# Attention outputs transposed in 32x32 blocks on VectorE instead of on TensorE, in a three-attention block on one core

## The chip, the core and the metric

The kernel runs as one program on one core of a Trainium2 chip. The core's engines run their own instruction queues and meet at semaphores: PE (TensorE, matrix products; PEld is its weight load), DVE (VectorE), ACT (ScalarE), POOL (GpSimd) and SP (SyncE, which here only issues DMAs). The metric is the device time of one execution in microseconds (us), lower is better.

## The reference

A batch of 16 sequences of 512 tokens with 128 channels goes through two layers, in fp32:

```python
x = L0_attn_x                                   # 16 x 512 x 128
xn = layernorm(x)
x = x + L0_attn(xn) + L0_ffn(xn)
xn = layernorm(x)
return x + L1_attn(xn) + L1_ffn(xn)
```

`L0_attn` ("A" in the kernel) has 16 query heads of 8 channels over 4 key/value heads, without a mask. `L0_ffn` contains a second attention ("M": 16 heads, keys and values from a normalised latent, rotary positions, causal) and then a mixture of 4 experts of which each token takes one. `L1_attn` ("B") has 16 query heads over one key/value head. `L1_ffn` is a gated feed-forward of width 384. Each attention computes `softmax(q k^T) v` per head, puts the heads' 8 channels side by side and multiplies by an output matrix `wo`.

## The kernel before, in words

One table of steps, written out by hand, sets the order of all work. `T` (L119) gives each step a place on a time axis, `stages` (L139) lists the steps of one sequence with their places, `ordered` (L225) folds the places modulo `PERIOD = 12` and sorts them, and each engine walks the folded table once per sequence, doing its own part of each step (`walk`, L434). So up to three sequences are in work at once, and the loop over sequences has 12 slots. `LATE` (L128) shifts a step on one engine alone. A place is only a rank: an engine's instructions run strictly in the order of the table, and wait there on semaphores.

The attentions take turns. In each slot one group of 4 heads is scored for its row maxima (`score_max`, L687 on PE, L956 on DVE), and another group, two slots behind, is scored again with the maximum folded in, exponentiated (`score_exp`, L707 on PE, L1201 on ACT) and multiplied with the values (`probs_v`, L723, PE). For A and B a group has 16 score_max units, each four matmuls in four column tiles into one PSUM bank and one DVE reduction of 128x512 (L966); for M the tiles grow with the causal row, and a masked reduction (L971) takes them. The slots with score_max of A are 8 to 11, of B 0 to 3, of M 4 to 7. The maxima go through POOL, PE, ACT and a DMA issued by SP (`shift_turn`, L560, L701, L1194) before the second scoring of that group.

PSUM has 8 banks: 7 that all score units and all small products take in turn (`misc_bank`, L604, waits for the last user of a bank), and one, `pv`, in which `probs_v` collects a pair of groups. After a pair of groups (twice per attention, so six times per sequence):

- `out_copy` (L1210): ACT copies `pv` (128x512) to `osb`. The `pv` bank is free again after it: `probs_v` of the next pair waits for it.
- `out_turn` (L742, L974): PE transposes `osb` in four 128x128 pieces into a PSUM bank, so that tokens lie on partitions; DVE takes the reciprocal of the row sums (L979) and multiplies (L986) into `otok`.

And once per attention, three times per sequence:

- `o_turn` (L749, L1216): PE transposes `otok` back in four 128x128 pieces, ACT copies the bank to `oT`; then `o_proj` (L754) multiplies with `wo`, and DVE adds the result (L998, L1002, L1006).

Other steps that the change moves: `m_lat_turn` (L646, L913: DVE normalises the latent, PE transposes it, DVE scales it), `gate`, `route` (L1032) and `scatter` (L1386) of the experts' routing, the POOL chains `split` with the nine `pack` DMAs behind each (L569), and the feed-forward `ff_up`, `ff_down`.

Of the kernel before, what the change touches and what calls it, by code (L numbers as in the profile page):

```python
# [31 lines left out]
ALU = mybir.AluOpType  # L32
# [3 lines left out]
P = 128  # L36
# [3 lines left out]
GROUP = 4  # L40
# [61 lines left out]
for _n, _w in (("a_bv", 32), ("a_bo", 128), ("gate_b", EXPERTS), ("b_bv", HD), ("b_bo", 128)):  # L102
# [16 lines left out]
T = dict(x_load=-0.9, x_norm=-0.066, res0=1.148, x_scaled=0.46, turn_xr=0.9, m_q=1.107, split_mq=1.25, m_lat=0.995,  # L119
         m_lat_turn=1.55, m_k=1.763, split_mk=1.85, m_v=1.95, turn_xn=2.283, a_q=2.542, split_aq=2.687, a_k=2.8,  # L120
         a_v=3.432, split_ak=3.649, pack=0.319, pack_a=1.414,
         nms=1.16, nmT=1.5, lag=1.986, pv_M=3.114, pv=3.265, out_copy=1.188, out_turn=0.125, o_turn=0.222, o_proj=0.382,
         x2_norm=0.352, e0=13.6, x2_scaled=-0.691, turn_r2=-0.5, gate=-0.318, ranks=0.157, route=0.15, route_step=0.043, scatter=0.75, xp_in=1.58, xp_turn=2.314, weights=1.15, wgap=0.209, wnext=0.2, up=2.849, step=0.248, later=0.3,
         y_out=0.25, gather=0.618, moe_added=1.272, down=0.03,
         b0=0.12, x1_scaled=0.177, res1=0.75, turn_x1=0.513, b_q=0.801, split_bq=0.18, b_k=1.03, split_bk=0.195, b_v=1.248,
         ff=1, ff_down=0.358)

LATE = {  # L128
    "SP": dict(shift_turn=0.067),
    "PE": dict(),  # L130
    "DVE": dict(o_proj=0.024, x1_scaled=0.022, m_lat_turn=0.0, x_scaled=-0.121, m_lat=0.0, x1_norm=0.0, x2_norm=0.0,
                down=0.0, out_turn=0.0, gate=0.0),
    "ACT": dict(turn=-0.056, out_copy=-0.063, o_turn=0.0, x_scaled=0.0, x2_scaled=0.0, shift_turn=0.017, m_v=0.0, up=-0.013),
    "POOL": dict(x_norm=0.106, x1_norm=0.184, x2_norm=0.042, m_lat=0.1, gate=0.1, m_q=0.069, m_k=0.05,
                 split=0.0, score_exp=0.0),
# [96 lines left out]
def spare_users(name, *args):  # L232
# [8 lines left out]
        "out_turn": [(f"{a}_otok", g + 1)] if name == "out_turn" else [],  # L241
        "o_turn": [(f"{a}_oT", 1)], "o_proj": [({"M": "x2_ready", "A": "gqa_added", "B": "y_ready"}.get(a), 1)],
# [12 lines left out]
def kernel_program(nc, x, w_all, w_lat, v_all, r_all, consts, wx, xq, yq, wi_up, wi_down, rope, out):  # L255
# [7 lines left out]
    with ctx:  # L263
# [63 lines left out]
        otok = sb("otok", [P, TILES, D])  # L327
# [63 lines left out]
        for a in "MBA":  # L391
# [206 lines left out]
        def _(pe):  # L598
# [143 lines left out]
            def out_turn(b, a, g):  # L742
                m = misc_bank(b, f"{a}_otok", g + 1)
                pe.wait_ge(sig[f"{a}_osb"], total(b, f"{a}_osb", g + 1))
                for t in range(TILES):
                    ins = pe.transpose(m[:, P * t:P * t + P], osb[:, g % 2, P * t:P * t + P], ident[:])  # L746
                ins.then_inc(sig[f"{a}_ot_ps"], 1)

            def o_turn(b, a):  # L749
                m = misc_bank(b, f"{a}_oT", 1)  # L750
                pe.wait_ge(sig[f"{a}_otok"], total(b, f"{a}_otok"))
                turns4(m, otok, f"{a}_oT_ps")

# [63 lines left out]
            def ff_down(b):  # L817
                m = misc_bank(b, "res_b", 1)
                pe.wait_ge(sig["ff_hid"], total(b, "ff_hid"))
                for t in range(TILES):  # L820
                    for c in range(FCH):
# [6 lines left out]
                         shift_turn=shift_turn, score_exp=score_exp, probs_v=probs_v, out_turn=out_turn,  # L828
                         o_turn=o_turn, o_proj=o_proj, gate=gate, ranks=ranks, xp_turn=xp_turn, up=up, down=down, ff_up=ff_up, ff_down=ff_down)
# [4 lines left out]
        def _(v):  # L834
            turn_mx, turn_full, turn_otok, turn_factored = {}, {}, {}, {}
            turn_hid = {}
# [279 lines left out]
            def ff_down(b):  # L1116
# [13 lines left out]
                         score_max=score_max, out_turn=out_turn, o_proj=o_proj,  # L1130
# [6 lines left out]
        def _(act):  # L1137
            turn_probs, turn_osb, turn_oT, turn_nmT, turn_factored = {}, {}, {}, {}, {}
# [71 lines left out]
            def out_copy(b, a, g):  # L1210
                act.wait_ge(sig[f"{a}_pv"], total(b, f"{a}_pv", len(CLUSTERS[a]) * (2 * g + 2)))
                for s_last, value in last_user(b, turn_osb, g % 2, f"{a}_ot_ps", g + 1):
                    act.wait_ge(s_last, value)
# [283 lines left out]
```

## Time and profile before

| | |
|---|---|
| median of 3 runs | 2818.49 us (2809.54 to 2819.48) |
| span of the profiled execution, first to last instruction | 2813.9 us |
| PE busy | 2628.6 us, 93% |
| PEld busy | 1437.3 us, 51% |
| DVE busy | 2305.2 us, 82% |
| ACT busy | 1727.4 us, 61% |
| POOL busy | 791.1 us, 28% |

The profiled execution is one of its own; of its time the trace has the span alone, which lies inside the range of the three runs and 4.6 us under their median. Matmuls overlap and their ends are modelled, so PE's busy time is an upper bound. The profile follows each idle stretch of an engine to the instruction that released it.

### The profile page before, as it was taken

The numbers are of one execution on the slowest core, as the hardware profiler recorded it, in microseconds if no ns is written. First come the engines' busy times: TensorE is split into PE (matmuls) and PEld (weight loads), VectorE is DVE, ScalarE is ACT, GpSimd is POOL, SyncE is SP. The second block draws the span as 40 slices with busy tenths as digits, with TensorE's granted clock in tenths as the row PEclk, the third lists the DMA queues.
The fourth block names the chain that finished last, engine by engine and source line by source line (L and its number), as shares of the span: only waits on it lengthen the run. The fifth ranks groups of instructions, "written<-read, shape, count | busy, mean of one in ns | idle before, by whom it ended". The sixth has DMA issues, their size and how long they took to land. (4 is left out here: it accounts for less than half of the span.)

```text
span 2813.9 us, 121706 instructions
## 1 busy us (share of the span) xinstructions
PE 2628.6 (93%) x51440; PEld 1437.3 (51%) x51440; DVE 2305.2 (82%) x6003; ACT 1727.4 (61%) x3522; POOL 791.1 (28%) x1369
## 2 busy tenths in 40 slices
PE   5969999999999999999999999999999999999958
PEld 2435454645546465464645546464554646546432
DVE  5758879798898979889797988979889897988825
ACT  1725756666576666757666575766657566675725
POOL 4132422223241222423223242222324122242110
PEclk7979999999999999999999999999999999999987
DMA  3041221403112041221304122140312214132120
GB/s 98 7 125 36 79 76 32 125 25 108 55 59 89 26 135 30 89 73 36 113 25 123 43 77 79 31 125 25 110 52 67 81 29 133 29 90 73 34 71 6
DMA packets 168048, 191.30 MB, mean 68 GB/s; under 512 B 24614, under 2 KB 150736, under 8 KB 167504
## 3 DMA queue, kind: packets, MB, share of 16 engines
q1 hardware_dynamic: 163408, 175.12, 20.4%
q0 software_dynamic: 4096, 8.40, 1.0%
q8 instruction: 406, 6.65, 1.0%
q14 instruction: 138, 1.13, 0.1%
HBM read 84.18 MB, written 16.25 MB: 36 GB/s over the span
## 5 line engine op out<-in xcount | busy, mean ns | idle before, releaser
L1208 ACT ACTIVATE probs<-bank 128x512 f32<-128x512 f32 x2688 | 1463.7, 599 | 678.2 <-PE bank L615 670.6
L966 DVE TENSOR_REDUCE mx<-bank 128x1 f32<-128x512 f32 x2048 | 1281.2, 682 | 62.4 <-PE bank L615 49.3
L971 DVE CUSTOM_DVE_ANT_0 bank<-bank,mask 128x128 f32<-128x128 f32 (+3 forms) x1024 | 478.5, 517 | 109.2 <-PE bank L615 101.7
L615 PE MATMUL bank<-kp_B,qp_B 72*32 72x512 bf16 x4096 | 439.9, 390 | 18.5 <-DVE mx L966 9.2
L615 PE MATMUL bank<-qp_B,kp_B 74*32 74x512 bf16 x4096 | 413.5, 382 | 3.1 <-ACT probs L1208 1.7
L615 PE MATMUL bank<-qp_A,kp_A 74*32 74x512 bf16 x4096 | 408.5, 380 | 6.8 <-DVE mx L966 6.2
L615 PE MATMUL bank<-kp_A,qp_A 72*32 72x512 bf16 x4096 | 394.8, 381 | 12.4 <-DVE mx L966 7.5
L615 PE MATMUL bank<-kp_M,qp_M 72*32 72x128 bf16 (+3 forms) x4096 | 318.4, 311 | 32.0 <-DMA kp_M<-parts_k 23.5
L1353 POOL TENSOR_SCALAR nms<-mx 128x16 bf16<-128x16 f32 x192 | 39.5, 206 | 1087.1 <-DVE mx L971 509.6
L615 PE MATMUL bank<-qp_M,kp_M 74*32 74x128 bf16 (+3 forms) x4096 | 297.5, 302 | 20.0 <-DVE mx L966 15.2
L736 PE MATMUL pv<-probs,vv_B 128*32 128x512 f32 x2048 | 274.8, 594 | 1.2 <-ACT probs L1208 1.0
L736 PE MATMUL pv<-probs,vv_A 128*32 128x512 f32 x2048 | 266.6, 593 | 0.1
L615 PEld LDWEIGHTS bank<-kp_B,qp_B 72*32 72x32 bf16 x4096 | 133.4, 97 | 207.0 <-issue 86.3
L615 PE MATMUL bank<-late_keys,identb 128*32 128x128 bf16 x4096 | 221.1, 221 | 0.9 <-issue 0.8
L615 PEld LDWEIGHTS bank<-qp_B,kp_B 74*32 74x32 bf16 x4096 | 129.8, 97 | 133.7 <-issue 51.7
L615 PEld LDWEIGHTS bank<-qp_A,kp_A 74*32 74x32 bf16 x4096 | 122.4, 97 | 147.4 <-DVE mx L966 42.6
L615 PEld LDWEIGHTS bank<-kp_A,qp_A 72*32 72x32 bf16 x4096 | 115.2, 96 | 146.4 <-DVE mx L966 58.9
L615 PEld LDWEIGHTS bank<-qp_M,kp_M 74*32 74x32 bf16 x4096 | 130.8, 97 | 108.1 <-DVE mx L966 40.0
L615 PEld LDWEIGHTS bank<-kp_M,qp_M 72*32 72x32 bf16 x4096 | 126.1, 99 | 108.3 <-issue 56.8
L736 PE MATMUL pv<-probs,vv_M 128*32 128x512 f32 (+3 forms) x2048 | 179.3, 437 | 0.2
L615 PEld LDWEIGHTS bank<-late_keys,identb 128*32 128x32 bf16 x4096 | 129.8, 98 | 50.1 <-issue 29.3
L971 DVE DVE_READ_ACCUMULATOR2_ANT mx<- 128x1 f32 x1024 | 145.2, 142 | 0.0
(167 smaller groups left out, 3286.4 us busy)
## 6 DMA issues: line engine op xcount, KB each, us to landing
wxs<-wx SPq DMA_DIRECT2D x112, 578.0 KB, 4.1
qp_M<-parts_q SPq DMA_DIRECT2D x144, 128.0 KB
kp_M<-parts_k SPq DMA_DIRECT2D x144, 128.0 KB
qp_A<-parts_q SPq DMA_DIRECT2D x144, 128.0 KB
qp_B<-parts_q SPq DMA_DIRECT2D x144, 128.0 KB
xp<-xq SPq DMA_DIRECT2D x16, 448.0 KB, 7.3
kp_A<-parts_k SPq DMA_DIRECT2D x144, 32.0 KB
xs<-x SPq DMA_DIRECT2D x16, 256.0 KB, 3.0
```

What stands on the lines that cost most here:

```text
L615: ins = pe.matmul(dst[at:at + n], lhsT[:, at:at + n], rhs, start=start, stop=stop, tile_position=(0, at))
L736: ins = pe.matmul(pv[0][32 * hh:32 * hh + VW, SEQ - q:SEQ], vv[a][:, c, VHEAD[a](GROUP * g + hh), :], probs[:, SLOT[a, g, u], col:col + q] ...
L966: v.tensor_reduce(mx[:, g % 2, at:at + 1], s1[BANK[a, g, u]][:], AX.X, ALU.max) \
L971: v.tensor_tensor_reduce(bank[:, 0:keys], bank[:, 0:keys], mask[:, SEQ - keys:SEQ], 1.0, LOWEST, ALU.add, ALU.max, mx[:, g % 2, at:at + 1] ...
L1208: act.activation(probs[:, slot, :], s2[BANK2[a, g, u]][:], ACT.Exp).then_inc(sig[f"{a}_exp"], 1)
L1353: chain(b, f"{a}_nms", 2 * g + 1, pool.tensor_scalar(first, top, 1.0, 0.0, ALU.mult, ALU.add))
```

## The change

The `pv` tile is transposed by DVE, and so is `otok`, each in one instruction over 128x512 that turns every 32x32 block in place. Head pairs lie on blocks of 32 partitions, so the blocks are enough: between the two transpositions a token's place within its block lies on the partition. The division reads `osb` in SBUF instead of a PSUM bank. PE and ACT have no part in `out_copy`, `out_turn` and `o_turn` any more, and the nine uses of the turning banks per sequence are gone. The rows of `wo` are put in another order on the host.

```diff
-        "out_turn": [(f"{a}_otok", g + 1)] if name == "out_turn" else [],
-        "o_turn": [(f"{a}_oT", 1)], "o_proj": [...
+        "o_proj": [...
...
-        otok = sb("otok", [P, TILES, D])
+        otok = sb("otok", [P, SEQ])
...
 # on PE: out_turn and o_turn are taken out
-            def out_turn(b, a, g):
-                m = misc_bank(b, f"{a}_otok", g + 1)
-                pe.wait_ge(sig[f"{a}_osb"], total(b, f"{a}_osb", g + 1))
...
-            def o_turn(b, a):
...
 # on DVE
+            def out_copy(b, a, g):
+                v.wait_ge(sig[f"{a}_pv"], total(b, f"{a}_pv", len(CLUSTERS[a]) * (2 * g + 2)))
+                for s_last, value in last_user(b, turn_osb, g % 2, f"{a}_otok", g + 1):
+                    v.wait_ge(s_last, value)
+                v.transpose(osb[:, g % 2, :], pv[0][:]).then_inc(sig[f"{a}_osb"], 1)
+
             def out_turn(b, a, g):
-                v.wait_ge(sig[f"{a}_ot_ps"], total(b, f"{a}_ot_ps", g + 1))
-                m = misc[SPARE[f"{a}_otok", g + 1]][:].rearrange("p (t h c) -> p t h c", t=TILES, c=VHALF)
+                v.wait_ge(sig[f"{a}_osb"], total(b, f"{a}_osb", g + 1))
+                m = osb[:, g % 2, :].rearrange("p (k h c) -> p k h c", h=2, c=VHALF)
...
                 v.reciprocal(r, m[:, :, :, HD]).then_inc(sig[f"{a}_rc"], 1)
...
+                dst = otok[:].rearrange("p (k g h d) -> p k g h d", g=TWOS, h=2, d=HD)[:, :, g]
+                v.tensor_tensor(dst, m[:, :, :, 0:HD], r.unsqueeze(3).broadcast_to([P, SEQ // TILE, 2, HD]), ALU.mult) \
+                    .then_inc(sig[f"{a}_otok"], 1)
+
+            def o_turn(b, a):
+                v.wait_ge(sig[f"{a}_otok"], total(b, f"{a}_otok"))
+                for s_last, value in last_user(b, turn_oT, 0, f"{a}_o_ps", 1):
+                    v.wait_ge(s_last, value)
+                v.transpose(oT[:], otok[:]).then_inc(sig[f"{a}_oT"], 1)
...
 # on ACT: out_copy and o_turn are taken out
-                act.activation(osb[:, g % 2, :], pv[0][:], ACT.Copy).then_inc(sig[f"{a}_osb"], 1)
...
-                act.activation(oT[:], misc[SPARE[f"{a}_oT", 1]][:], ACT.Copy).then_inc(sig[f"{a}_oT"], 1)
```

The steps' places also change. In `T` (before, after; the others stay):

```
turn_xr 0.9 0.81    m_q 1.107 1.103      m_lat 0.995 0.943   m_k 1.763 1.724     split_mk 1.85 1.774
m_v 1.95 1.813      res0 1.148 1.007     x_load -0.9 -0.923  x_scaled 0.46 0.579 a_k 2.8 2.963
a_v 3.432 3.374     split_ak 3.649 3.654 nmT 1.5 1.422       o_turn 0.222 0.162  e0 13.6 13.621
turn_r2 -0.5 -0.399 route_step 0.043 0.053  xp_turn 2.314 2.341  weights 1.15 1.141  wgap 0.209 0.168
moe_added 1.272 1.279  turn_x1 0.513 0.459  b_q 0.801 0.601  split_bq 0.18 0.281  b_k 1.03 1.118
split_bk 0.195 0.245   b_v 1.248 1.83       ff 1 1.199       ff_down 0.358 0.346
```

and `LATE` becomes

```python
    "SP": dict(shift_turn=0.351, y_out=0.008, xp_in=0.021, pack=0.082),
    "PE": dict(m_v=-0.035, o_proj=-0.027, m_lat_turn=0.123, b_v=-0.004, ranks=-0.104, a_q=-0.077, turn=-0.047,
               down=-0.019),
    "DVE": dict(o_proj=0.024, x1_scaled=0.022, x_scaled=-0.121, x2_norm=-0.155, down=-0.031, out_turn=0.131,
               route=0.1, m_q=0.001, x_norm=0.039),
    "ACT": dict(turn=-0.037, out_copy=-0.081, x_scaled=0.01, shift_turn=0.017, up=-0.013, a_k=0.291, b_q=0.501),
    "POOL": dict(x_norm=0.051, x1_norm=0.184, x2_norm=0.042, m_lat=0.1, gate=-0.056, m_q=0.069, m_k=-0.063,
               res1_start=-0.147, scatter=-0.042, res0_start=0.015),
```

(before: SP `shift_turn=0.067`; PE nothing; DVE `o_proj`, `x1_scaled`, `x_scaled` as now and zeros; ACT `turn=-0.056, out_copy=-0.063, shift_turn=0.017, up=-0.013`; POOL `x_norm=0.106, x1_norm=0.184, x2_norm=0.042, m_lat=0.1, gate=0.1, m_q=0.069, m_k=0.05`). Folded to the 12 slots, PE's part of `m_lat_turn` goes from 2.550 to 2.673 while DVE's stays at 2.550; the expert gate's POOL part goes ahead of the `split` of M's queries; SP's part of `shift_turn` goes 0.2 slots back, behind `pack` or `weights` issues in slots 2, 3, 6 and 10; the feed-forward goes 0.2 slots back.

## Rows read from the trace of the kernel before

**Rows 1.** The page: span; busy time by engine, share, instructions.
```profile
span 2813.9 us, 121706 instructions
PE 2628.6 (93%) x51440; PEld 1437.3 (51%) x51440; DVE 2305.2 (82%) x6003; ACT 1727.4 (61%) x3522; POOL 791.1 (28%) x1369
```
**Rows 2.** Timeline, DVE: start, length, one instruction that runs once per sequence, ten apart.
```profile
492.55 0.45 DVE L1052 TENSOR_TENSOR past<-first_row,cst 1x21 f32<-1x21 f32 x1
2160.63 0.45 DVE L1052 TENSOR_TENSOR past<-first_row,cst 1x21 f32<-1x21 f32 x1
```
**Rows 3.** Windows, slots 0-2, 2-4, 4-8, 8-12: length; PE, PEld, DVE, ACT, POOL busy.
```profile
1449.90:1474.10 24.20, 23.32 (x366) 10.72 (x362) 22.91 (x47) 19.70 (x43) 3.81 (x11) 1.00 0.01 2
1474.10:1507.60 33.50, 32.32 (x563) 16.38 (x552) 30.32 (x70) 20.70 (x43) 21.39 (x32) 1.00 0.28 84
1507.60:1561.10 53.50, 52.35 (x1305) 34.95 (x1307) 39.08 (x157) 34.41 (x73) 8.45 (x16) 1.00 0.43 133
1561.10:1616.70 55.60, 53.80 (x1014) 27.40 (x1010) 51.29 (x105) 33.05 (x63) 15.23 (x26) 1.00 0.12 33
```
**Rows 4.** Waits in 1561.1 to 1616.7: who waited for whom, us, times, longest.
```profile
PEld bank L615 <- DVE mx L966: 7.3, 17, 1.1
DVE res L1119 <- PE bank L615: 1.5, 1, 1.5
```
**Rows 5.** Timeline, 1508.0 to 1512.6: one end of a pair of groups.
```profile
1509.88 0.60 ACT L1214 ACTIVATE osb<-pv 128x512 f32<-128x512 f32 x1 [0.29 <-PE pv L736]
1510.63 0.63 PE L746 MATMUL bank<-ident,osb 128*128 128x128 f32 x4 [0.21 <-ACT osb L1214]
1511.19 0.29 PE L615 MATMUL bank<-kp_M,qp_M 72*32 72x256 bf16 x4
```
**Rows 6.** Timeline, PE, 1483 to 1486: the transposition of the latent.
```profile
1485.14 0.60 PE L650 MATMUL bank<-ident,latn 128*64 128x128 f32 x4 [1.18 <-DVE latn L859]
```
**Rows 7.** Timeline, DVE, 1480 to 1487: four reductions in a row.
```profile
1481.59 2.47 DVE L966 TENSOR_REDUCE mx<-bank 128x1 f32<-128x512 f32 x4
```
**Rows 8.** Groups by line: count, busy us, mean ns, idle before.
```profile
L1214 ACT ACTIVATE osb<-pv 128x512 f32<-128x512 f32 x96 | 57.3, 597 | 61.8 <-PE pv L736 61.7
L1220 ACT ACTIVATE oT<-bank 128x512 f32<-128x512 f32 x48 | 28.0, 584 | 15.2 <-PE bank L621 15.2
L1096 DVE TENSOR_TENSOR acc<-acc,moe 128x512 f32<-128x512 f32 x16 | 10.9, 682 | 9.1 <-DMA moe<-yq,row_at_i 9.1
L923 DVE TENSOR_SCALAR latT<-bank,vec 64x512 f32<-64x512 f32 x16 | 12.8, 801 | 12.9 <-PE bank L650 12.9
```
**Rows 9.** Timeline, SP, 1483 to 1508: DMA issues.
```profile
1484.96 6.01 SPq L584 DMA_DIRECT2D qp_M<-parts_q  x9
1501.79 1.21 SPq L566 DMA_DIRECT2D qp_B<-nmT  x2
```
**Rows 10.** DMA issues of the whole span: KB each, median us to landing.
```profile
xp<-xq SPq DMA_DIRECT2D x16, 448.0 KB, 7.3
qp_A<-nmT SPq DMA_DIRECT2D x128, 4.0 KB, 1.7
```
**Rows 11.** Timelines, POOL, SP and PE, 1480 to 1522: routing, scatter and what reads it.
```profile
1484.16 0.20 POOL L1378 TENSOR_SCALAR oneh<-eq 128x4 f32<-128x4 f32 x1
1485.87 0.20 POOL L1384 TENSOR_TENSOR oneh<-eq,seen 128x4 f32<-128x4 f32 x1
1499.37 1.11 POOL L1394 DMA_INDIRECT xq<-factored,row_at_i  x1 [1.95 <-DVE row_at_i L1072]
1508.06 0.39 SPq L530 DMA_DIRECT2D xp<-xq  x1
1518.04 0.66 PE L788 MATMUL bank<-ident,xp 128*128 128x128 f32 x4
```
**Rows 12.** Timeline, 2800 to 2814: the end of the last sequence.
```profile
2805.24 0.60 ACT L1214 ACTIVATE osb<-pv 128x512 f32<-128x512 f32 x1 [1.19 <-PE pv L736]
2809.02 1.54 PE L615 MATMUL bank<-w,oT 128*32 128x128 f32 x32 [0.78 <-ACT oT L1220]
```

More of the change, by code:

```diff
@@ L115 @@
             "B": ((0, 4), (4, 8), (8, 12), (12, 16))}
[L119 to L126, printed above, removed]
@@ L128 @@
-LATE = {
[L129 to L135, printed above, removed]
+T = dict(x_load=-0.923, x_norm=-0.066, res0=1.007, x_scaled=0.579, turn_xr=0.81, m_q=1.103, split_mq=1.25,
+         m_lat=0.943, m_lat_turn=1.55, m_k=1.724, split_mk=1.774, m_v=1.813, turn_xn=2.283, a_q=2.542,
+         split_aq=2.687, a_k=2.963, a_v=3.374, split_ak=3.654, pack=0.319, pack_a=1.414, nms=1.16, nmT=1.422,
+         lag=1.986, pv_M=3.114, pv=3.265, out_copy=1.188, out_turn=0.125, o_turn=0.162, o_proj=0.382, x2_norm=0.352,
+         e0=13.621, x2_scaled=-0.691, turn_r2=-0.399, gate=-0.318, ranks=0.157, route=0.15, route_step=0.053,
+         scatter=0.75, xp_in=1.58, xp_turn=2.341, weights=1.141, wgap=0.168, wnext=0.2, up=2.849, step=0.248,
+         later=0.3, y_out=0.25, gather=0.618, moe_added=1.279, down=0.03, b0=0.12, x1_scaled=0.177, res1=0.75,
+         turn_x1=0.459, b_q=0.601, split_bq=0.281, b_k=1.118, split_bk=0.245, b_v=1.83, ff=1.199, ff_down=0.346)
@@ L240, in spare_users @@
         "shift_turn": [(f"{a}_nmT", g + 1)] if name == "shift_turn" else [],
-        "out_turn": [(f"{a}_otok", g + 1)] if name == "out_turn" else [],
-        "o_turn": [(f"{a}_oT", 1)], "o_proj": [({"M": "x2_ready", "A": "gqa_added", "B": "y_ready"}.get(a), 1)],
+        "o_proj": [({"M": "x2_ready", "A": "gqa_added", "B": "y_ready"}.get(a), 1)],
         "gate": [("logits", 1)],
@@ L827, in _ @@
                          a_q=a_q, a_k=a_k, a_v=a_v, b_q=b_q, b_k=b_k, b_v=b_v, score_max=score_max,
-                         shift_turn=shift_turn, score_exp=score_exp, probs_v=probs_v, out_turn=out_turn,
-                         o_turn=o_turn, o_proj=o_proj, gate=gate, ranks=ranks, xp_turn=xp_turn, up=up, down=down, ff_up=ff_up, ff_down=ff_down)
+                         shift_turn=shift_turn, score_exp=score_exp, probs_v=probs_v, o_proj=o_proj, gate=gate, ranks=ranks, xp_turn=xp_turn, up=up, down=down, ff_up=ff_up, ff_down=ff_down)
             walk(steps, ordered(LATE["PE"]))
@@ L1129, in _ @@
                          b_v=lambda b: value(b, "B", "b_ps", "b_bv", "bv_ready"),
-                         score_max=score_max, out_turn=out_turn, o_proj=o_proj,
+                         score_max=score_max, out_copy=out_copy, out_turn=out_turn, o_turn=o_turn, o_proj=o_proj,
                          x2_norm=x2_norm, gate=gate, route=route, up=up, down=down, moe_added=moe_added,
@@ L1208, in score_exp @@
                 act.activation(probs[:, slot, :], s2[BANK2[a, g, u]][:], ACT.Exp).then_inc(sig[f"{a}_exp"], 1)
[L1210 to L1213, printed above, removed]
-                act.activation(osb[:, g % 2, :], pv[0][:], ACT.Copy).then_inc(sig[f"{a}_osb"], 1)
-            def o_turn(b, a):
-                act.wait_ge(sig[f"{a}_oT_ps"], total(b, f"{a}_oT_ps"))
-                for s_last, value in last_user(b, turn_oT, 0, f"{a}_o_ps", 1):
-                    act.wait_ge(s_last, value)
-                act.activation(oT[:], misc[SPARE[f"{a}_oT", 1]][:], ACT.Copy).then_inc(sig[f"{a}_oT"], 1)
             def xp_turn(b, half):
@@ L1251, in _ @@
                            m_v=m_v, shift_turn=shift_turn,
-                           score_exp=score_exp, out_copy=out_copy, o_turn=o_turn, xp_turn=xp_turn, up=up,
+                           score_exp=score_exp, xp_turn=xp_turn, up=up,
                            ff_up=ff_up), ordered(LATE["ACT"]))
@@ L1434 @@
     k_at = {"A": HD * (np.arange(KCH["A"]) % KV0) + np.arange(KCH["A"]) // KV0, "B": np.arange(KCH["B"])}
[L1436 removed]
+    head, pair, odd, ch_of = np.unravel_index(np.arange(D), (GROUP, TWOS, 2, HD))
     o_at = HD * (GROUP * (2 * pair + odd) + head) + ch_of
```

21 lines of the change are left out of this document (4 added, 17 removed).

## The prediction, made before the changed kernel was built or run

> **What bounds the kernel now.** I read the page first: PE is busy 93% of the span, DVE 82%, ACT 61% [rows 1]. Then the length of a period: one DVE instruction that runs once per sequence stands at 492.55 and, ten sequences on, at 2160.63, so a period is 166.8 us [rows 2]. The reader is to see next, in the windows of one period, that the bound is not the same everywhere [rows 3]. In slots 4 to 8 PE is busy 52.35 of 53.5 us while DVE idles 14.4 and ACT 19.1: PE alone sets the pace. In the other three stretches (113.3 us together) PE is busy 109.4, but DVE is busy 104.5 and idles only 8.8 (1.3, 3.2 and 4.3), and PE waits for it: 7.3 us on its weight loads in slots 8 to 12, always for a reduction that has to free a bank [rows 4]. There two engines are nearly full side by side. The change takes work from the one and gives it to the other.
>
> The Trainium skill ("Trainium Kernel Development and Optimization", Performance Expectations) calls matmul busy time a bad measure and weight-load busy time a good one. By that PE, at 51%, would be far from its limit and lose nothing by these transpositions. In slots 4 to 8 the trace speaks against it: no other engine is near full there. It stands behind the rival of no change.
>
> **What PE loses.** Nine sets of four transpositions per period: six `out_turn`, three `o_turn`. From the start of one set to the next product 0.56 us pass (1510.63 to 1511.19) [rows 5]; 9 x 0.56 = 5.0 us. By their places: one set in slots 0 to 2, two in 2 to 4 (A's last), three in 4 to 8 (B's last), three in 8 to 12 (M's last).
>
> **What ACT loses.** Nine copies of 0.60 us, 5.3 us per period [rows 8]. ACT idles in every stretch [rows 3]; taken as nothing, at most the 0.21 us that PE stood before a set [rows 5].
>
> **What DVE gains.** Nine transpositions over 128x512, six from PSUM, three from SBUF. The trace has none, so I bound it by other instructions of that size: reductions from PSUM follow each other at 0.60 us ((2.47 - 0.68) / 3, the last one taken as long as a lone instruction of that size) [rows 7]; an addition in SBUF takes 0.68 alone, and the slowest one of 512 columns, a scaling from PSUM, 0.80 [rows 8]. I take 0.60, as the nearest in kind (one source from PSUM, one element after the other, in a queue): 5.4 us per period, 0.6, 1.2, 1.8 and 1.8 by stretch. That a block needs more than one pass is the last rival below. The division keeps its 32 and 256 elements and reads SBUF in place of PSUM: nothing, within 0.1 us either way.
>
> On this price the Trainium skill has a rule ("VectorE: DVE Perf Modes", The three transpose paths): 311 ns on VectorE for 128x128, 390 on TensorE, and its rules for authors give a 128x128 transposition to TensorE. Four times 311 is 1.24 us by that page, an estimate, twice my 0.60, and by it the change costs DVE 11.2 us. No run so far shows it.
>
> **The sum by stretch.** Slots 4 to 8: PE gives back 3 x 0.56 = 1.7 us, and DVE's 39.1 + 1.8 stays far below 51.8; -1.7.
>
> The other three: PE falls to 109.4 - 6 x 0.56 = 106.1, and with its present idle time of 3.9 the stretches could shrink to 110.0. DVE rises to 104.5 + 3.6 = 108.1, and with its present idle time of 8.8 they would grow to 116.9. What decides is how much of DVE's idle time is slack. A part are waits on PE that get shorter when DVE runs later than PE (1.5 us before adding the feed-forward's result [rows 4]); a part are hand-overs in chains (latent, feed-forward) that stay. I let half stay: 108.1 + 4.4 = 112.5; -0.8.
>
> **The places.** `m_lat_turn`: PE stands 1.18 us before it, for DVE's normalised latent [rows 6]. Its PE part goes 0.123 slots back, in slots of 16.75 us (33.5 / 2 [rows 3]) 2.1 us; but on DVE two new instructions (1.2 us) come ahead of it in that slot. So 0.3 of the wait could stay and 0.9 go. Behind it `m_k` now follows closer, and waits for the scaled latent, an instruction of 0.80 [rows 8]. I take -0.4, with bounds of 0 and -0.9.
>
> SP's part of `shift_turn`, two DMAs: for B's third group it was issued from 1501.79 to 1503.00 [rows 9] and lands 1.7 us after [rows 10], 2.9 before slot 4 opens at 1507.6, where PE reads it. Now the last two packs (6.01 / 9 = 0.67 each [rows 9]) and two weight loads go ahead of it, some 2 us. 0.9 is left, so nothing; without that cover PE would wait 1 to 2 us per period. In the other slots what goes ahead is less or the slot longer.
>
> POOL's gate, seven instructions from 1484.16 to 1486.07 [rows 11], goes ahead of the split of M's queries, and the nine packs behind it end some 2 us later than 1490.97 [rows 9], for a slot that opens at 1507.6: nothing. The twelve `route` steps spread up to 0.23 slots further back, 3.9 us; POOL's scatter, which waits for the last of them already (1.95 us), follows, then the load of the sorted rows, which lands 7.3 us [rows 10] after 1508.06, at 1515.4, 2.7 before PE reads it at 1518.04 [rows 11]. PE's reading goes back by 0.05 slots, 0.8. That is 3.5 against 3.9: nothing taken, up to +0.4. Feed-forward 0.2 slots back: in the half above. `b_v`, 0.58 back, is read four slots later.
>
> **The new wait.** In `out_copy` DVE waits for PE's last product into `pv`, with its reductions queued behind, and PE needs the banks that they free. ACT stood so 61.7 us over 96 copies, 0.64 each [rows 8]. I count nothing extra, since DVE in the full stretches arrives late, not early, and in slots 4 to 8 has room. The other way, PE's next pair waits until DVE has emptied `pv`. Its first product lies 0.235 slots behind `out_copy` in the table for A and B, some 3 us in slots of 12 to 14 us; DVE, at most some four reductions (2.4 us) behind before PE runs out of banks, and 0.6 for the transposition, just keeps that.
>
> **Total.** -1.7 - 0.8 - 0.4 = -2.9 us per period. 15 periods stand between the 16 sequences: -43.5. At the very end, where nothing covers the chain from 2805.24 to the last projection at 2809.02 [rows 12], two sets and two copies (2 x (0.63 + 0.60) [rows 5]) give way to two transpositions of 0.68: -1.1. 2813.9 - 44.6 = 2769.3 for the span; the median of the runs is 4.6 us above the span shown: 2774.
>
> **The rivals.**
> - PE alone counts: DVE's new work disappears in its idle time, the three stretches shrink to 110.0 and the latent's wait by 0.9. -1.7 - 3.3 - 0.9 - 0.4 (ACT's copies no longer waited for) = -6.3, so 2723. For it: PE is at 93% everywhere. Against: PE waits for DVE's reductions already.
> - No change: 6.5 of DVE's 8.8 us turn out to be hand-overs; the three stretches grow by 1.3, which with the latent's 0.4 eats the 1.7: 2817.
> - Slower: DVE stands at `pv` as ACT did, 0.64 us at each of four ends outside slots 4 to 8, 2.6 us, so that its idle time stays at 8.8 although it runs later. 116.9 in place of 113.3, the latent's wait unchanged: +3.6 - 1.7 = +1.9 per period, 2846. It turns slower from the point where 6.9 us of idle time stay. For it: ACT's idle time before the copies was all for PE [rows 8]. Against: [rows 4].
> - A transposition takes two passes, 1.20 us: DVE 111.7 in the three stretches, with half the idle time 116.1, +2.8, -1.7 in slots 4 to 8, the latent's wait stays: +1.1, 2834. By the skill's 1.24 it would be the same within 5 us.
>
> **Chances.** Forecast 0.50, with a range of its own of 2737 to 2803 (a quarter to three quarters of DVE's idle time stay); PE alone 0.14; no change 0.15; DVE at `pv` 0.12; two passes 0.09. 0.5%, 14 us, is what a measurement here can tell from no change. Faster by more: 0.46 of the forecast, 0.14, and 0.05 of the third, 0.65. Within: 0.04 + 0.08 + 0.04 of the slower ones, 0.16. Slower: 0.19. The range runs from 2720, which takes in most of the second case, to 2840, between the two slow ones.
>
> **What would show it.** Right: DVE busy up by some 5 us per period to about 149, transpositions at 0.60 to 0.70, PE down to about 157 of 164; slots 4 to 8 near 51.8 us, the others near 112; no wait of PE for `osb` above some tenths. Wrong: transpositions above 1 us; DVE idle before `out_copy` for PE's product; PE idle before the second scoring for a DMA of `nmT`; slots 8 to 12 longer than 55.6; or slots 4 to 8 unchanged, which would mean that PE was not their bound.

## The result and the profile after

The changed kernel takes 2825.64 us (median of 20 runs), the kernel before in the same runs 2817.38: ratio 1.0031, 95% interval 1.0021 to 1.0040. 2774 us had been forecast; it became slightly slower. The page of the changed kernel, span and busy times [rows 1]:

```profile
span 2829.3 us, 120408 instructions
PE 2587.7 (91%) x50864; PEld 1427.0 (50%) x50864; DVE 2377.3 (84%) x6147; ACT 1692.9 (60%) x3378; POOL 799.1 (28%) x1369
```

The work moved: PE has 41 us less, DVE 72 more. Yet the span is 15 us longer, so PE stands more. Windows of one period of the changed kernel, the same four stretches [rows 3]; the number before the DMA share is the granted clock:

```profile
1457.60:1482.00 24.40, 23.31 (x362) 9.51 (x362) 23.29 (x48) 19.59 (x41) 5.06 (x12) 1.00 0.01 3
1482.00:1514.60 32.60, 30.50 (x542) 14.28 (x535) 30.73 (x71) 20.52 (x42) 17.62 (x28) 1.00 0.28 84
1514.60:1571.50 56.90, 51.09 (x1301) 34.99 (x1297) 41.27 (x162) 33.38 (x71) 11.59 (x19) 1.00 0.42 125
1571.50:1626.20 54.70, 51.97 (x998) 28.46 (x991) 52.49 (x107) 32.15 (x60) 15.09 (x25) 1.00 0.12 33
```

Slots 2 to 4 and 8 to 12 are 0.9 us shorter each, slots 4 to 8 are 3.4 longer, though PE is busy 1.3 less there. Taken as means over 11 periods, from the first `score_max` product of a slot to that of the next, the period goes from 166.8 to 167.9: slots 0 to 2 from 24.2 to 24.5, 2 to 4 from 33.7 to 33.1, 4 to 8 from 53.2 to 55.3, 8 to 12 from 55.6 to 54.9. The loss sits in slot 4 (11.5 to 13.7) and slot 6 (18.5 to 18.7, where it should have shrunk). All slot and period lengths below are such means; a wait "per period" is the time by which PE's products start later than those before them allow, by what released them, over 12 periods.

Waits of the whole span of the changed kernel (us, times, longest) name two candidates:

```profile
PEld bank L613 <- DMA qp_B<-nmT: 32.1, 17, 3.1
PE bank L613 <- DMA qp_B<-nmT: 23.9, 15, 2.5
PE bank L613 <- DMA wxs<-wx: 22.4, 30, 1.8
DVE osb L964 <- PE pv L734: 45.9, 50, 14.7
PE bank L648 <- DVE latn L845: 24.9, 16, 3.1
```

The wait for B's `nmT` is new, and the one for the expert weights `wxs` was shorter before:

```profile
PE bank L615 <- DMA wxs<-wx: 8.7, 9, 1.9
```

The chain of waits of the changed kernel goes through that shift DMA once in nearly every period (14 such steps, 3.6 to 7.1 us); two of them:

```profile
1514.11 4.01 DMA qp_B<-nmT
2344.88 4.85 DMA qp_B<-nmT
```

The operations themselves are near the forecast (groups of DVE: count, busy us, mean ns, idle before; the mean is that of a whole instruction, which in a queue runs into the next one):

```profile
L964 DVE STREAM_TRANSPOSE osb<-pv 128x512 f32<-128x512 f32 x96 | 68.3, 711 | 45.9 <-PE pv L734 45.9
L984 DVE STREAM_TRANSPOSE oT<-otok 128x512 f32<-128x512 f32 x48 | 33.8, 703 | 0.1
L977 DVE TENSOR_TENSOR otok<-osb,rc 128x256 f32<-128x256 f32 x96 | 44.1, 460 | 3.3
L971 DVE RECIPROCAL rc<-osb 128x32 f32<-128x32 f32 x96 | 32.8, 342 | 0.1
```

### The profile page after: what moved, and what is told of

It is laid out like the page before. It is cut to its first block, busy times and chain, and to the rows that moved or that the text cites. A ratio compares the mean times of both kernels' runs of the same rounds, so it can differ in the third digit from the quotient of the medians.

```text
span 2829.3 us, 120408 instructions
## 1 busy us (share of the span) xinstructions
PE 2587.7 (91%) x50864; PEld 1427.0 (50%) x50864; DVE 2377.3 (84%) x6147; ACT 1692.9 (60%) x3378; POOL 799.1 (28%) x1369
## 3 DMA queue, kind: packets, MB, share of 16 engines
q1 hardware_dynamic: 163408, 175.12, 20.6%
## 4 chain that ended last, share of the span: by engine, by line
PE 45%; DVE 29%; issue 7%; SPq 7%; DMA 6%; POOL 5%; ACT 2%; POOLq 0%; DVEq 0%; ACTq 0%
PE bank L613 33%; DVE mx L952 16%; PE pv L734 10%; SPq L582 4%; DMA wxs<-wx 3%; DMA qp_B<-nmT 2%; SPq L536 2%; DVE bank L957 1%; ACT probs L1204 1%; DVE osb L964 1%; POOL sq L1282 1%; DVE bn L827 1%; PE bank L619 1%; DVE oT L984 1%; DVE latn L845 1%
## 5 line engine op out<-in xcount | busy, mean ns | idle before, releaser
L613 PE MATMUL bank<-kp_B,qp_B 72*32 72x512 bf16 x4096 | 421.8, 391 | 18.7 <-DVE mx L952 9.8
L613 PE MATMUL bank<-qp_A,kp_A 74*32 74x512 bf16 x4096 | 417.1, 382 | 8.8 <-DVE mx L952 8.2
L613 PE MATMUL bank<-kp_A,qp_A 72*32 72x512 bf16 x4096 | 403.5, 383 | 6.7 <-DVE mx L952 3.4
L613 PE MATMUL bank<-kp_M,qp_M 72*32 72x128 bf16 (+3 forms) x4096 | 327.6, 317 | 32.7 <-issue 27.6
L613 PE MATMUL bank<-qp_M,kp_M 74*32 74x512 bf16 (+3 forms) x4096 | 299.9, 305 | 17.7 <-DVE mx L952 15.8
L613 PEld LDWEIGHTS bank<-qp_A,kp_A 74*32 74x32 bf16 x4096 | 128.1, 96 | 186.7 <-DVE mx L952 106.1
L613 PEld LDWEIGHTS bank<-kp_M,qp_M 72*32 72x32 bf16 x4096 | 132.3, 101 | 110.2 <-issue 72.2
L613 PEld LDWEIGHTS bank<-kp_A,qp_A 72*32 72x32 bf16 x4096 | 122.7, 96 | 119.1 <-DVE mx L952 42.5
L613 PE MATMUL bank<-xpT,wxs 128*32 128x128 f32 x3584 | 124.6, 277 | 26.6 <-DMA wxs<-wx 22.4
```

Of the source, the lines that this page charges most:

```text
L613: ins = pe.matmul(dst[at:at + n], lhsT[:, at:at + n], rhs, start=start, stop=stop, tile_position=(0, at))
```

## The experiments

### Exchange and places apart

**e1**: the changed code with the old places.

```diff
-T = dict(x_load=-0.923, ...   # after
+T = dict(x_load=-0.9, ...     # before
-LATE = ...                    # after
+LATE = ...                    # before
```

> The transpositions are on VectorE as in the changed kernel, but all steps have the places of the kernel before (T and LATE of before). Theory P (the exchange of engines gains what was forecast, the new places take it back): PE's stalls return from 17.1 to about 12 us per period, the waits for DMA nmT (1.9), for the expert weights (1.4), for POOL's nms (1.0) go to a few tenths; time 2760 to 2785, ratio to before about 0.98 to 0.99. Theory D (DVE is the bound, and its 5.4 us of new work eat the 5.0 us that PE loses, whatever the places): 2810 to 2835, ratio 1.00 +- 0.005, and the stalls of PE on DVE's reductions rise by 3 us per period or more.

2881.29 us, ratio 1.0259 (1.0238 to 1.0280). The period is 171.6, and nearly all of the loss lies in slot 2, 20.6 to 24.9. Neither theory had this: with the old places the exchange loses.

**e2**: the code of before with the new places.

```diff
-T, LATE = ...   # before
+T, LATE = ...   # after
```

> The transpositions stay on PE and ACT as in the kernel before, but all steps have the new places (T and LATE of the changed kernel). Theory P: the new places by themselves cost some 3 to 5 us per period, 2860 to 2895. Theory D: the places are about neutral, 2810 to 2830.

2883.82 us, 1.0254 (1.0230 to 1.0278). In the kernel before the two waits below come to 9.0 and 2.2 us. DVE's division frees the turning bank, and with the new places it comes later:

```profile
PEld bank L616 <- DVE otok L987: 80.0, 74, 1.8
PE bank L616 <- DVE otok L987: 49.3, 74, 1.4
```

Each half alone costs some 2.5%, together 0.3%: the places belong to the exchange, and no part of the result can be read as one half's share.

**e7**: e1 with `m_lat_turn`'s new place on PE.

```diff
-    "PE": dict(),
+    "PE": dict(m_lat_turn=0.123),
```

> e1_old_places (transpositions on VectorE, all places as before) with a single new place: PE's part of m_lat_turn 0.123 slots back, as in the changed kernel. Theory L (with the old places the whole loss is in slot 2, where DVE's three new steps of A come ahead of the latent and PE and DVE wait for each other in turn): slot 2 falls from 24.9 to 21 us, ratio to before 0.997 to 1.005. Theory D (DVE's load is the loss): no change, 1.02 or more.

2853.60 us, 1.0127 (1.0108 to 1.0145): half of e1's loss, between the two expectations. Slot 2 falls from 24.9 to 22.4.

### How much PE and DVE count

**e4**: the kernel before, each of the nine sets of PE transpositions done twice.

```diff
-                for t in range(TILES):
+                for t in (*range(TILES), *range(TILES)):
```

> The kernel before, with each of the nine sets of four PE transpositions per period done twice into the same place: prices PE's part. If 0.56 us of PE work per set is what the time pays (PE bound everywhere): 9 x 0.56 x 15 = +76 us, 2893. If only slots 4 to 8 are bound by PE: 3 x 0.56 x 15 = +25, 2842. If PE has room: 2817.

2854.20 us, 1.0158 (1.0136 to 1.0180). 5.0 us of PE work per period lengthen it by 2.1, 43%. The three sets in slots 4 to 8, 1.7 us, make that stretch 0.5 longer. In slot 6 PE's busy time grows by 0.7 and the slot by 0.1: PE is not its bound.

**e8**: e5 (below) with `out_copy`'s transposition done twice.

```diff
+                v.transpose(unused[:, g % 2, :], pv[0][:])
                 v.transpose(osb[:, g % 2, :], pv[0][:])...
```

> e5_shift with out_copy's transposition done twice (once into a tile that nothing reads): prices six DVE transpositions per period, 6 x 0.6 = 3.6 us. If DVE's time is on the path in slots 0 to 4 and 8 to 12, four of six count: +2.4 us per period, +36 us on e5_shift. If everywhere: +54. If DVE has room: within 10 us.

2822.29 us, 1.0030 (1.0016 to 1.0043), 28 above e5. In a queue one takes 673 ns, alone 711; from the start of the first to that of the second pass 0.64 us:

```profile
L965 DVE STREAM_TRANSPOSE unused<-pv 128x512 f32<-128x512 f32 x96 | 68.2, 711 | 33.3 <-PE pv L735 33.3
L966 DVE STREAM_TRANSPOSE osb<-pv 128x512 f32<-128x512 f32 x96 | 64.6, 673 | 0.0
```
```profile
1454.18 0.72 DVE L965 STREAM_TRANSPOSE unused<-pv 128x512 f32<-128x512 f32 x1 [0.25 <-PE pv L735]
1454.82 0.67 DVE L966 STREAM_TRANSPOSE osb<-pv 128x512 f32<-128x512 f32 x1
```

The period grows by 2.2 of the 3.8 added (6 x 0.64), 2.0 of it outside slots 4 to 8, where four of the six lie (2.6 us).

### The shift of the maxima on SP

**e3**: the changed kernel with all of SP's old offsets.

```diff
-    "SP": dict(shift_turn=0.351, y_out=0.008, xp_in=0.021, pack=0.082),
+    "SP": dict(shift_turn=0.067),
```

> The changed kernel, with only SP's shifts (LATE of SP) as before: shift_turn 0.067 in place of 0.351, no shift of pack, xp_in and y_out. Theory P: PE's wait for the DMA of nmT into qp_B at the opening of slot 4 (1.9 us per period) goes, and part of the wait for the expert weights: 2785 to 2805. Theory D: PE waits for DVE instead, 2820 to 2830.

2810.50 us, 0.9998 (0.9987 to 1.0010). Slot 4 is back (13.7 to 11.3), but slot 8 grows from 11.5 to 13.3. There the second `y_out` now stands behind a shift on SP; POOL's gather of the experts' rows waits for it, and POOL's maxima stand behind that gather. PE's wait for them in e3, and in the changed kernel:

```profile
PE bank L702 <- POOL nms L1338: 44.5, 29, 3.8
```
```profile
PE bank L702 <- POOL nms L1338: 11.4, 20, 1.3
```

**e5**: only the shift, and only so far that it is issued ahead of the last two packs.

```diff
-    "SP": dict(shift_turn=0.351, y_out=0.008, ...
+    "SP": dict(shift_turn=0.145, y_out=0.008, ...
```

> The changed kernel with one number of SP's shifts changed: shift_turn 0.145 in place of 0.351, so that SP's part stands at 0.567 of each slot, where it was in the kernel before, ahead of the last packs and of the expert weights; y_out and pack keep their new shifts. Theory S (SP's shift_turn, behind a weight load that waits for the routing, opens slot 4 late): PE's wait for the DMA of nmT, 1.9 us per period, goes; slot 4 falls from 13.7 to about 11.3 us, nothing comes back in slot 8; ratio to before 0.985 to 0.992. Theory Q (the time of slot 4 is lost somewhere else as soon as this wait goes, as it seemed with all of SP's shifts undone): ratio 0.997 to 1.003.

2793.75 us, 0.9919 (0.9905 to 0.9933): 32 us less, period 165.9, slot 4 at 11.3, the wait for `nmT` from 1.86 to 0.16 us per period. The moved shift costs more than the 8 us by which the changed kernel is slower than the one before. What on SP makes it late, three runs had to tell. SP in the changed kernel (start, length):

```profile
1504.61 6.27 SPq L582 DMA_DIRECT2D kp_M<-parts_k  x9
1513.09 0.36 SPq L537 DMA_DIRECT2D wxs<-wx  x1
1513.50 1.20 SPq L564 DMA_DIRECT2D qp_B<-nmT  x2
```

From the end of the packs at 1510.88 to the weight load pass 2.2 us without a DMA. The first explanation: the weight load waits for a routing step, and `route` was moved back.

**e11**: `route` at its old places.

```diff
-          ... route_step=0.053,
+          ... route_step=0.043,
-               route=0.1, m_q=0.001, ...
+               m_q=0.001, ...
```

> The changed kernel with the twelve routing steps of DVE put back to their old places (LATE of route gone, route_step 0.043 again), SP's shift left at 0.351. Theory S1 (the shift is late because the weight load ahead of it on SP waits for a routing step that was moved back too): the semaphore comes some 3 us earlier, when the packs have just been issued, so PE's wait for nmT falls from 1.86 us per period to below 0.5, slot 4 from 13.7 to 12 or less, the time by 20 to 32 us, ratio 0.992 to 0.996. Rival S2 (two packs and a weight load ahead of the shift are too much by themselves, whatever route does): nmT wait stays above 1.2, time within 8 us of the changed kernel, ratio 1.000 to 1.006.

2824.16 us, 1.0035 (1.0015 to 1.0055): nothing. In e11 SP stands just as long, 1497.94 to 1499.89, though DVE wrote the experts' numbers at 1490.66:

```profile
1490.95 6.99 SPq L582 DMA_DIRECT2D kp_M<-parts_k  x9
1499.89 0.36 SPq L537 DMA_DIRECT2D wxs<-wx  x1
1500.31 1.20 SPq L564 DMA_DIRECT2D qp_B<-nmT  x2
```
```profile
1490.66 0.15 DVE L1057 CAST tile_expert_i<-tile_expert 1x7 int32<-1x7 f32 x1
```

So it is no semaphore. What is left in those lines of code is the read of the expert's number into a register of SP (`value_load`), and the weights' 578 KB ahead of the shift's 4.

**e13**: the shift and the weight load, neighbours on SP, change places.

```diff
-          ... weights=1.141,
+          ... weights=1.155,
```

> The changed kernel with one pair of neighbours exchanged on SP: the first expert-weight load of a sequence (weights at 1.155 in place of 1.141) now stands just behind the shift of B's third group, not just ahead of it; two packs stay ahead. Theory V (what makes the shift late is that weight load, 2.6 us from the end of the packs at 1510.88 to the shift at 1513.50, most of it without a DMA, while SP reads the expert's number into a register): the shift goes out 2.6 us earlier, PE's wait for nmT falls from 1.86 us per period to below 0.5, slot 4 from 13.7 to 11.3 to 11.8, the time by 25 to 33 us, ratio 0.992 to 0.995. Rival Q (the two packs, or ACT's shifted maxima themselves, are late enough): nmT wait above 1.2, time within 8 us of the changed kernel.

2785.49 us, 0.9907 (0.9892 to 0.9921), slot 4 at 11.5, `nmT` wait 0.09 us per period. The shift now follows the packs at once:

```profile
1485.86 6.18 SPq L582 DMA_DIRECT2D kp_M<-parts_k  x9
1492.08 1.24 SPq L564 DMA_DIRECT2D qp_B<-nmT  x2
1494.88 0.36 SPq L537 DMA_DIRECT2D wxs<-wx  x1
```

**e14**: the order of the changed kernel, the register load left out for the first tile.

```diff
-                e = sp.value_load(tile_expert_i[0:1, j:j + 1], ...)
+                e = sp.value_load(tile_expert_i[0:1, j:j + 1], ...) if j else 0
...
```

> The changed kernel with its places, but the first weight load of a sequence takes expert 0 as a constant instead of reading the expert's number into a register (left out: the choice of the first tile's expert). Theory V (the register load is the price, some 2.2 of the 2.6 us): the weight load costs SP only its 0.36 us, the shift goes out some 2 us earlier, nmT wait below 0.7 us per period, slot 4 at 12 or less, the time 18 to 32 us below the changed kernel, ratio 0.992 to 0.997. Rival R (the 578 KB of the weights occupy the DMA engines ahead of the 4 KB of the shift): the exchange of places gains, this edit does not; nmT wait above 1.2. Rival Q: neither gains.

2809.19 us, 0.9991 (0.9978 to 1.0004): 0.4% of e13's 1.2%, slot 4 at 12.7, between the two theories. SP, and the product that waited:

```profile
1488.69 5.21 SPq L582 DMA_DIRECT2D kp_M<-parts_k  x8
1494.00 0.55 SPq L537 DMA_DIRECT2D wxs<-wx  x1
1494.59 1.39 SPq L564 DMA_DIRECT2D qp_B<-nmT  x2
```
```profile
1500.28 0.40 PE L613 MATMUL bank<-qp_B,kp_B 74*32 74x512 bf16 x4 [0.74 <-DMA qp_B<-nmT]
```

The gap of 2 us is gone: it was the read into the register. That read has a row of its own if its line is asked for; the changed kernel's 112 reads (ns: shortest, median, longest):

```profile
L536 SPq TENSOR_LOAD <-tile_expert_i x112: 263/442/1648, 165.1 to 2713.8; - x112
```

The 15 reads right behind a pack of `kp_M` took 1.14 to 1.65 us, the 45 right behind the smaller packs of `kp_A` 0.44 to 0.95, the 16 right behind the load of `xp` 0.26 to 0.28. About 0.5 us of register instructions follows each. Why a read behind packs is long is not shown.

But the shift, issued to the end by 1495.98, frees PE only at 1500.28, more than 4 us later. The 1.7 us of [rows 10] is no measure for it: that is the shift of A. The trace has every DMA packet, and by their sizes the shift's packets can be told from the weights'. All times here are means over eleven sequences. From the start of its issue to its last packet, B's shift took 3.6 us in the kernel before and in e13, with only packs ahead, 3.9 in the changed kernel, and 5.4 in e14. In e14 it was issued nearly as early as in e13, 4.4 us ahead of slot 4 against 4.7, but its last packet ran 1.1 us after the slot opened, not 1.1 before; its packets began and ended behind those of the weights. In the changed kernel the last packet ran 1.7 us after the opening. So both theories hold: of the 2.9 us by which e13 brings the last packet forward, leaving out the read gives 0.7, and the rest is put down to the 578 KB ahead.

### The expert weights

**e6**: e5 with four weight buffers.

```diff
-WSLOTS, HSLOTS = 3, 3
+WSLOTS, HSLOTS = 4, 3
```

> e5_shift with four places for the experts' weights in place of three (WSLOTS 4), so that a load starts one expert tile earlier. Theory W (slot 6 is bound by the loads of the expert weights, so that PE's saved 1.1 us there turned into waiting): slot 6 falls from 18.7 to 17.5 us or less, 15 to 25 us less than e5_shift. If slot 6 is bound by the hand-overs up, hid, down instead: within 5 us of e5_shift.

2752.65 us, 0.9774 (0.9757 to 0.9792), period 163.4, slot 6 from 19.1 to 16.6.

**e9**: the same edit in the kernel before. **e10**: in the changed kernel, its shift left late.

> The kernel before with four buffers for expert weights in place of three; nothing else. Theory W2 (the expert-weight loads lay just under PE's own work in slot 6 of the kernel before and became the bound there only when PE had less to do): in the trace of before PE's products wait for wxs some 0.24 us per period and stall 1.33 us in slot 6 in all, so 4 to 16 us go: ratio 0.994 to 0.999, a third or less of the 41 us that the same edit took from the changed kernel. Rival X (a fourth buffer is worth its 41 us whatever the transpositions do, and it has nothing to do with the lost prediction): ratio near 0.985, slot 6 shorter by 2 us or more.

2793.90 us, 0.9920 (0.9905 to 0.9935): 23 us, between the two expectations. Slot 6 goes from 18.5 to 17.4, so a part of this bound was there before, more than its 0.24 us per period of waits for `wxs` showed; another part appears only when PE has less to do (19.1 to 16.6 from e5 to e6).

> The changed kernel with four buffers for expert weights, SP's shift of the maxima left late. If the two losses in slots 4 and 6 are independent, the time is that of the changed kernel less 41 us: near 2785, ratio 0.987 to 0.991, slot 4 still 13.5 to 14 us, slot 6 near 16.6. If they are linked (the wait at slot 4 gives the weight loads time, or the fourth load stands ahead of the shift as well), slot 4 grows above 14 and the time is 2795 or more.

2790.27 us, 0.9882 (0.9849 to 0.9915): the two losses add up. Slots 4 to 8 in one period of e6, then of e9:

```profile
1475.80:1526.20 50.40, 50.16 (x1301) 35.06 (x1297) 41.15 (x161) 33.55 (x71) 11.35 (x19) 1.00 0.46 141
```
```profile
1493.80:1545.70 51.90, 51.41 (x1304) 34.54 (x1307) 38.84 (x157) 34.24 (x73) 8.32 (x16) 1.00 0.46 133
```

With a fourth buffer PE is busy nearly throughout in both, and only then, and with the shift mended, do the transpositions taken from it shorten this stretch, by 1.5 us here and 1.3 in the mean.

**e12**: e6 with two more places undone.

```diff
-          ... nmT=1.422,          "PE": dict(... turn=-0.047, ...
+          ... nmT=1.5,            "PE": dict(...
```

> The changed kernel with SP's shift at 0.145 and four weight buffers, and two more places undone: nmT at 1.5 again (POOL's nms was waited for 0.99 us per period) and PE's own shift of the turns gone (waits for DVE and ACT at the turns' places, 1.17 us per period). If half of these 2.1 us counts: some 15 us below the 2753 of the kernel without them, ratio 0.971 to 0.974. If these waits only change places: 2745 to 2760, ratio 0.975 to 0.980.

2760.97 us, 0.9801 (0.9788 to 0.9815): the waits change places. That for POOL's maxima falls from 0.74 to 0.25 us per period, those for DVE's reductions rise from 5.75 to 6.44, and the time is 8 us above e6.

### The clock of TensorE

e1's wait for the latent is 1.6 us per period longer than before, its slot 2 is 4.3 longer. Windows of e1 in slot 2, first the whole slot, then single microseconds; then PE there:

```profile
1511.60:1536.30 24.70, 20.48 (x377) 9.68 (x369) 20.55 (x49) 10.30 (x21) 11.94 (x20) 0.86 0.16 50
1521.60:1522.60 1.00, 0.27 (x8) 0.00 (x0) 1.00 (x3) 0.60 (x1) 0.67 (x5) 1.00 0.05 8
1522.60:1523.60 1.00, 0.00 (x0) 0.00 (x0) 1.00 (x3) 0.00 (x0) 0.74 (x4) 0.50 0.22 41
1527.60:1528.60 1.00, 1.00 (x8) 0.16 (x4) 0.20 (x1) 0.53 (x1) 0.00 (x0) 0.50 0.51 160
1529.60:1530.60 1.00, 1.00 (x76) 0.86 (x72) 0.95 (x2) 0.60 (x1) 0.00 (x0) 1.00 0.42 140
```
```profile
1524.62 1.03 PE L647 MATMUL bank<-ident,latn 128*64 128x128 f32 x4 [2.75 <-DVE latn L844]
```

Here the granted clock falls to 0.50 (1.2 GHz) while PE stands, and it stays there for nearly 5 us after the work has come back: the four transpositions take 1.03 us in place of 0.60 [rows 6]. In each of e1's 11 periods the clock falls during this wait or within 0.7 us behind it. The kernel before never has it: 1.00 in each slot of these periods. The changed kernel has it in some periods; the same slot with and without (slot 2, slot 9, and slot 4 at its worst, behind the wait for `nmT`):

```profile
1980.30:2000.30 20.00, 18.22 (x369) 9.22 (x365) 18.79 (x44) 11.08 (x24) 11.26 (x19) 1.00 0.13 37
1310.00:1333.00 23.00, 21.23 (x365) 9.75 (x361) 18.67 (x44) 11.09 (x24) 11.55 (x20) 0.85 0.18 52
1582.90:1600.80 17.90, 17.04 (x291) 9.15 (x287) 16.82 (x30) 8.05 (x15) 9.33 (x12) 1.00 0.18 53
1240.90:1260.10 19.20, 18.36 (x291) 10.14 (x287) 17.10 (x30) 8.14 (x15) 9.32 (x12) 0.91 0.17 52
2346.20:2366.30 20.10, 17.61 (x203) 8.21 (x195) 11.37 (x39) 9.78 (x18) 7.24 (x10) 0.66 0.48 150
```

What is missing to 1.00, times the slot's length, is the clock's share. It is an upper bound of what the clock costs, since it counts time at 0.50 in which PE stands anyway. It comes to 1.56 us per period in the changed kernel (0.77 in slot 4, 0.63 in 2, 0.16 in 9), 3.30 in e1, 1.10 each in e5, e6 and e7, 1.87 in slot 8 of e3, nothing in e4 and e9. The Trainium skill ("TensorE: Matmul & The Clock Gate", HAM oscillation) says that PE standing for DMAs can lose its clock again and again; the last row, behind a wait of 2.49 us for a DMA, agrees. Whether the fall is a loss of its own or only goes with the waiting, work that nobody needs can tell.

**e15** (in e1), **e16** (in the changed kernel), **e17** (in e6): throw-away transpositions in PE's holes, ahead of the wait. In e16 PE also waits for the bank before it waits for the shift, so that the filling stands between the two.

```diff
+            def keep_busy(m, n):
+                for _ in range(n):
+                    pe.transpose(m[:, 0:P], ident[:], ident[:])
...
                 m = misc_bank(b, "latT_ready", 1)
+                keep_busy(m, 12)        # 5 in e16 and e17
                 pe.wait_ge(sig["latn_ready"], ...
...
+                if what == "x1":        # e16 and e17
+                    keep_busy(m, 3)
...
+                if (a, g, u) == ("B", 2, 0):        # e16
+                    keep_busy(s2[BANK2[a, g, u]], 6)
```

> The new transpositions at the old places (as e1), and PE multiplies twelve throw-away 128x128 transpositions of a constant into the bank of the latent before it waits for the latent: about 1.8 us of added PE work per period, all of it inside PE's hole of 2.75 us in slot 2. Theory C (in e1 that hole makes the granted clock of TensorE fall to 0.50 for some 7 us in every period, which is 3.3 of the 4.9 us that e1 loses): with the hole filled the clock stays at 1.00, slot 2 falls from 24.9 to 21.5 to 22.5 us, the time by 35 to 50 us against e1, ratio 1.007 to 1.014. Rival D (the wait itself is the loss, the clock only goes with it): PE has more to do and waits for the same latent, slot 2 stays near 25, ratio 1.024 or more.

2853.61 us, 1.0149 (1.0129 to 1.0169): 31 us below e1 by the ratios, with 1.5 us more PE work in every period. Slot 2 goes from 24.9 to 22.5, the clock's share from 3.30 to 0.15. A slot 2 of e15, and PE in it:

```profile
1318.10:1340.60 22.50, 19.86 (x387) 10.60 (x378) 20.29 (x49) 10.18 (x22) 12.07 (x20) 1.00 0.18 56
```
```profile
1328.30 1.53 PE L618 MATMUL bank<-ident 128*128 128x128 f32 x12
1330.98 0.63 PE L652 MATMUL bank<-ident,latn 128*64 128x128 f32 x4 [1.15 <-DVE latn L849]
```

> The changed kernel with throw-away transpositions of a constant on PE in three of its holes: five before the wait for the latent (slot 2), six before the second scoring of B's third group (slot 4, the wait for nmT), three before the turn of x1 (slot 9); 14 of 0.15 us, 2.1 us of added PE work per period. Theory C (the granted clock falls in some periods after these holes, worth 1.56 us per period by the windows): the clock stays at 1.00, period 167.9 to 166.3 to 167, time 12 to 23 us below the changed kernel, ratio 0.995 to 0.999. Rival D: the added work costs, or hides in the holes and changes nothing: ratio 1.002 to 1.010.

2804.61 us, 0.9964 (0.9948 to 0.9980): 0.7% below the changed kernel, though in slots 4 and 6 the clock still falls in four of eleven periods, for 0.93 us per period in place of 1.56.

> The best kernel so far (the changed kernel, SP's shift at 0.145, four weight buffers) with five throw-away transpositions before the wait for the latent and three before the turn of x1. Theory C: the 1.10 us per period of falls of the clock that its windows show in slots 2 and 9 go, time 8 to 16 us below the 2753 of that kernel, ratio 0.971 to 0.975. Rival D: no gain, ratio 0.977 to 0.982.

2736.71 us, 0.9721 (0.9703 to 0.9739), the best version, 16 us below e6. The clock is at 1.00 in all eleven periods, the period 162.2.

## Why the prediction was wrong

The sum gave -2.9 us per period, and +1.1 came. Forecast and measured by its steps:

- **Slots 4 to 8, "PE alone sets the pace", -1.7: +2.1 came.** This is the step that failed, and it failed twice: here and by the shift of the next point. I had read PE's 52.35 busy us of 53.5 as a bound. But 1.7 us more of PE work there cost 0.5 (e4). In slot 6 the pace was set by the expert weights: PE's busy time fell by 0.9 us there, its idle time rose by 1.1, and with a fourth buffer the idle time went (e6, e9).
- **"SP's part of `shift_turn` ... 0.9 is left, so nothing": 2.2 us in slot 4.** In the mean of eleven sequences the shift was issued 6.0 us ahead of slot 4 and is now 2.2 ahead. Of these 3.9 I had counted 2: the issue times. Not counted was the gap of 2 us at the register read before a weight load. The landing was taken at the 1.7 us of A's shift; B's, behind packs, takes 3.6 to its last packet, and 3.9 with the weights ahead. So 2.4 us of cover became 1.7 us of delay. The price without cover, "1 to 2 us", was right in size; that the cover was gone I did not see. The gap stood in the trace of before too, between the end of the packs at 1504.42 and the weight loads (SP, start and length):

```profile
1503.04 1.38 SPq L584 DMA_DIRECT2D kp_M<-parts_k  x2
1506.39 1.56 SPq L539 DMA_DIRECT2D wxs<-wx  x2
```

- **A term that the sum lacked: TensorE's clock**, at most 1.56 us per period in the changed kernel, none before (e15 to e17).
- **The other three stretches, -0.8 and -0.4 for the latent: -1.0 came** (24.2 + 33.7 + 55.6 to 24.5 + 33.1 + 54.9), with at most 0.8 of the clock's loss in it. That this is near the forecast is partly luck. I had let half of DVE's 8.8 us of idle time stay; 5.8 stayed, two thirds. And DVE's busy time there grew by 1.9 us, not by 3.6, since the new places moved work into slots 4 to 8 (with the old places, e1, it grew by 4.2). Of 2.6 us of DVE work added there in e8, 2.0 appear, 0.6 of them by a larger clock share. The latent's wait itself did not shrink, 1.31 to 1.56 us per sequence (21.0 and 24.9 over 16); the step's new place only keeps the exchange from lengthening it (e1, e7).
- **The transposition, 0.60: 0.71 and 0.70 as an instruction, 0.64 from one to the next (e8)**, which is what the 0.60 was taken from; far from the 1.20 of two passes. Both rivals on DVE are out: two passes, and a stand at `pv`, where DVE waited 45.9 us, 14.7 of it once at the end, against ACT's 61.7. By the Trainium skill ("VectorE: DVE Perf Modes", The three transpose paths) 1.24 was the estimate, four times its 311 ns for 128x128 in bf16; the trace disagrees. The Trainium skill's rule of weight-load busy time ("Trainium Kernel Development and Optimization", Performance Expectations), read as that PE at 51% has nothing to lose, is half right: added PE work cost 43% of itself (e4).
- **The end, -1.1: -1.3**, from 3.78 us [rows 12] to 2.45. Behind it the last projection takes 1.93 us in place of 1.54: PE stands 2.5 us before it, and its clock is at 0.63 in the mean over the 4 us around it.
- **The rival of no change** has a slip: it counts the latent's 0.4 as a loss, where the sum has it as a gain.

With the shift mended, four buffers on both sides and the clock kept (e17 against e9) exchange and places together are worth 165.6 - 162.2 = 3.4 us per period, with 1.2 us of throw-away work in e17; the forecast was 2.9. In slots 4 to 8 it is 1.7, as forecast, once PE sets the pace there. So the size was about right where its conditions were met. The exchange has no price by itself: with the old places it costs 4.9 (e1). Not settled is why a register read behind packs is long, and why the clock falls in some periods of a slot and not in others.

## What to carry to other kernels

Of a DMA issue that is moved past others, count what the queue does between two issues, a read into a register above all, and the bytes queued ahead of it, not the issue times alone. Take its landing time from the same DMA at the same place, not from one like it. Before an engine is called the bound of a stretch, look for its waits there, or add work to it and see whether the stretch grows. Work taken from TensorE makes holes; look at the granted clock behind each new hole, and where it falls, shorten the hole or fill it.

## What the runs showed of the hardware

Reading one number from SBUF into a register of SP held its queue for 0.26 to 1.65 us, and some 0.5 us of register instructions followed; right behind the 128 KB packs of `kp_M` it was never under 1.1 (all in the changed kernel). The timeline of SP leaves these instructions out: there only the gap shows them. The 32x32-block transposition of 128x512 fp32 takes DVE 0.67 us in a queue and 0.70 to 0.71 alone, from PSUM as from SBUF, about what a reduction of that size takes (0.68); the next instruction can start 0.64 us after it. Two 4 KB DMAs behind a 578 KB one on the same queue took 5.4 us from the start of their issue to their last packet (e14), and 3.6 without it (e13), in both with packs ahead. The Trainium skill ("DMA: Bandwidth & Descriptors", Queues, rings and completion order) has each DMA engine take a queue's descriptors in order; the small packets began and ended behind the large ones, which agrees, though the records do not tell the engines apart. TensorE's clock, once down to 0.50, stayed there for nearly 5 us of nearly full work in the case of e1 shown above and for 13 us in the worst one (a mean of 0.66 over 20.1 us); and the same wait of 0.72 us in slot 9 was followed by a fall in some periods and not in others.
